# The base inverse of a gated delta-rule kernel: its DVE sections placed at other slots, and one ACT copy between two Silus

## The chip, the cores and the metric

One core of one Trainium2 chip runs the whole program. The time is that of one execution on the device, in microseconds, as the median of several runs. The engines are TensorE (PE, with its weight loads shown as PEld), VectorE (DVE), ScalarE (ACT), GpSimd (POOL) and SyncE (SP). Each has its own queue, runs it in order, and is tied to the others by semaphores alone.

## The reference, cut to what matters

The program is a block of four layers. Only the first, an attention layer with a gated delta rule over 32 value heads, is touched:

```python
mixed = silu(causal_conv4(x @ w_qkv))            # q, k: 16 heads; v: 32 heads
beta, g = sigmoid(x @ w_b), -exp(A_log) * softplus(x @ w_a + dt_bias)
def step(state, inp):                            # over 1024 tokens
    state = state * exp(g_t)
    delta = (v_t - k_t @ state) * b_t
    state = state + outer(k_t, delta)
    return state, q_t @ state
core = norm_w * rms(core) * silu(z)
return core @ w_out
```

A scan, two quantized feed-forward layers and a state-space layer follow (the last quarter of the time); the change leaves them alone.

## The kernel before

**Units and slots.** The layer is cut into 32 units (2 batches by 16 key heads, 2 value heads each) and each unit's 1024 tokens into 8 chunks of 128. A unit starts every 8 slots. `for slot in range(ATTENTION_SLOTS)` runs over 279 slots, and each engine's function (`tensor`, `scalar`, `vector`, `gpsimd`, `sync`) walks the same slots and issues what is due in each: a step of unit n that is written for unit slot k is issued in slot 8n+k. Several units are in flight, so a slot is known by its **position**, its number modulo 8; unit slots 9 and 17 both fall on position 1. In every slot there is one step of the scan over chunks (unit slots 16 to 23), up to three products of the projection ("a", "b", "c" in the code, L676) and one output product (L831).

**The scan's step in a slot.** PE multiplies key and state (L712); DVE makes the residual from it (`resid`, L1333); PE multiplies that with the triangular inverse (L780) to `u`, which ACT copies (L1046); PE makes the state's update and the output (L810, L814); DVE takes them into `state` (L1406) and `o` (L1417). At a unit's chunk 0 there is no residual and the copies are L1399 and L1414.

**The inverse.** Each unit needs the inverse of 8x2 triangular 128x128 tiles, in two halves a=0 and a=1. The 16x16 diagonal blocks are inverted on DVE by `base_inverse`: section 0 is four 32x32 transposes and four elementwise steps (L1167 to L1178), and then for each column j from 1 to 14 three short dependent instructions on 128 x 8j elements (shuffle L1186, multiply L1188, add L1190), with one more (L1194) at the end. POOL spreads the result over the blocks (`inv`, L1519, "the mask"). DVE turns that (`turn_base`, L1198), and PE takes it from there: L605, which waits for the mask, then L608, which waits for DVE's turned copy and for ACT's copy of L605's result (`off`, L1068), and further levels in the next slots, of which L617 waits for ACT's copies L1074/L1075.

**Where the sections stand before.** Half 0: section 0 at unit slot 10, columns 1 to 6 at 11 ahead of the state, columns 7 to 10 at the end of slot 11, columns 11 to 14 at the end of slot 12. Half 1: the same four slots later, with section 0 at the end of slot 14. So the last columns stand right ahead of the residual of position 5 (half 0) and of position 1 (half 1).

**Other work named below.** `evict_pair` (L1150, L1153) and `subtract` (L1371, in the old code inline) prepare the decay matrix; `gate_out` writes `oT` (L1291) after PE's transposes (L761); `convolve` is three passes of L1306 over 128x1024, which wait for ACT's first tap (L1008); L1277 on DVE and L910, L914 and L917 on ACT read the projection's products out of the banks. On POOL, L1460 sums weights, L1498 scales `o`, L1505 masks the decay and L1469 issues the output's DMA. In ACT's queue, positions 1 and 5 have a table load (L1016), two Silus (L888), the copies, a Silu on `z` (L1051), a table load back (L1052) and then L1068.

Of the kernel before, what the change touches and what calls it, by code (L numbers as in the profile page):

```python
# [13 lines left out]
P = 128  # L14
# [200 lines left out]
def attention(nc, ctx, c, banks, dram, x_in, x_out, early):  # L215
    on = signals(nc, ctx, ATTENTION_SIGNALS)
    with ExitStack() as st:
# [631 lines left out]
        def scalar(e):  # L849
# [92 lines left out]
            for slot in range(ATTENTION_SLOTS):  # L942
# [72 lines left out]
                if n_qk is not None or n_v is not None or n_z is not None:  # L1015
                    e.preload_act_table_set(SILU_SET)  # L1016
                    if n_qk is not None:
                        silu(n_qk, K)
                        silu(n_qk, Q)
                    if n_v is not None:  # L1020
                        silu(n_v, V0)
                        silu(n_v, V1)
                    if n_z is None:
                        e.preload_act_table_set(EXP_SET)

                if slot in (5, 6):
                    evict_rows(1, range(4 * (slot - 5), 4 * (slot - 4)))
                read_at(slot, "b")
# [109 lines left out]
        def vector(e):  # L1138
# [16 lines left out]
            def base_inverse(n, a, section):  # L1155
# [24 lines left out]
                for j in range(1, BASE - 1):  # L1180
                    if section == (1 if j < 7 else 2 if j < 11 else 3):
# [10 lines left out]
                if section == 3:  # L1192
# [101 lines left out]

            def convolve(slot, taps):
# [18 lines left out]
            for slot in range(ATTENTION_SLOTS):  # L1314
# [33 lines left out]

                for a in range(2):
                    n = unit_at_only(slot, 9 + 4 * a)  # L1350
                    if n is not None:
                        evict_pair(n, a, 0)
                for a in range(2):
                    n = unit_at_only(slot, 8 + a)
                    if n is not None:
                        N = n
                        if a == 0:
                            if N in (0, HK):
                                e.wait_ge(on["gates"], N // HK + 1)
                            e.wait_ge(on["ln"], N + 1)  # L1360
                            if N > 0:
                                e.wait_ge(on["decay_sub"], 2 * N)
                            norm = ln_norm[:, N % 3, K, :].unsqueeze(1).broadcast_to([P, REP, NC])
                            heads = slice(REP * (n % HK), REP * (n % HK + 1))
                            e.tensor_tensor(col_beta[:, :, :], gc_beta[:, n // HK, heads, :], norm, ALU.add).then_inc(
                                on["col_beta"], 1)
                        e.wait_ge(on["chunk_exp"], 2 * N + a + 1)
                        e.wait_ge(on["col_beta"], N + 1)
                        dec = decay_half(N, a)
                        col = col_beta[:, :, HALF * a:HALF * (a + 1)].unsqueeze(3).broadcast_to([P, REP, HALF, P])  # L1370
# [1083 lines left out]
```

## Time and profile before

| | us |
|---|---|
| median of 3 runs (lowest to highest) | 4165.66 (4164.44 to 4167.02) |
| the profiled execution | 4168.05 |
| its span, first to last instruction | 4166.1 |
| attention with both scan and projection running, one unit | 88.2 |
| PE busy / DVE / ACT / POOL in the span | 3997.3 / 3196.9 / 2592.6 / 958.8 |

Times in the trace are microseconds from the span's start. The unit whose slots are quoted below is typical: from the second unit to the last but one, a unit took 88.14 to 88.58 us, but for the second (88.36) and the thirtieth (87.82), and the steps stand at the same distances in each. The granted TensorE clock is 0.991 of full speed over the span.

### The profile page before, as it was taken

The page shows a single profiled execution, that of the slowest core. Times are in us where ns is not written, and L with a number is a line of the kernel's source. Part 1 is how long each engine was busy: PE and PEld are TensorE (multiplying, and loading weights), DVE is VectorE, ACT ScalarE, POOL GpSimd, SP SyncE. Part 2 cuts the span into 40 slices and gives each one's busy share as a digit, 9 for nine tenths or more (in the row PEclk, how much of TensorE's full clock was granted, in tenths as well). Part 3 has the DMA queues.
Part 4 walks back from the last instruction along what each step waited for, and adds up shares of the span by engine and source line. Part 5 has one row for each costly group of instructions (what it writes and reads, how often), then busy time and mean ns, then how long its engine had stood idle before and what let it go on. Part 6 is the DMA issues. An engine that isn't in the chain of part 4 may idle for free. (4 is left out here: it accounts for less than half of the span.)

```text
span 4166.1 us, 83038 instructions
## 1 busy us (share of the span) xinstructions
PE 3997.3 (96%) x29437; PEld 2282.0 (55%) x29437; DVE 3196.9 (77%) x8334; ACT 2592.6 (62%) x6087; POOL 958.8 (23%) x1110
## 2 busy tenths in 40 slices
PE   7999999999999999999999999998899999999999
PEld 4555556556555555566565555555444444444444
DVE  4777887787787777877778877777447989898940
ACT  3566676666666666666666666666445656574643
POOL 1224333234333243333333333332100000000000
PEclk9999999999999999999999999999999999999999
DMA  3223334333433433343334333334304545454510
GB/s 131 83 72 84 87 86 90 85 80 85 92 77 85 120 82 85 90 86 85 81 87 92 75 87 85 82 80 97 83 1 132 164 148 168 147 175 153 183 57 10
DMA packets 290733, 402.99 MB, mean 97 GB/s; under 512 B 25774, under 2 KB 125362, under 8 KB 290258
## 3 DMA queue, kind: packets, MB, share of 16 engines
q1 hardware_dynamic: 253458, 330.57, 26.1%
q0 software_dynamic: 36864, 67.13, 12.0%
q8 instruction: 236, 3.87, 0.4%
q14 instruction: 175, 1.43, 0.1%
HBM read 288.56 MB, written 113.25 MB: 96 GB/s over the span
## 5 line engine op out<-in xcount | busy, mean ns | idle before, releaser
L676 PE MATMUL bank<-x_blocks,rows_b 128*128 128x512 f32 x1536 | 713.0, 597 | 0.9 <-ACT partial L914 0.9
L1306 DVE SCALAR_TENSOR_TENSOR conv<-raw,conv_w,conv 128x1024 f32<-128x1024 f32 x384 | 522.7, 1361 | 61.9 <-ACT conv L1008 56.8
L676 PE MATMUL bank<-x_blocks,w_pair 128*128 128x512 f32 x1152 | 549.9, 605 | 14.8 <-DVE x_blocks L1277 4.5
L831 PE MATMUL bank<-w_out_unit,oT 128*128 128x512 f32 x1008 | 491.4, 610 | 0.9 <-ACT out_stage L931 0.9
L676 PEld LDWEIGHTS bank<-x_blocks,rows_b 128*128 128x128 f32 x1536 | 274.9, 190 | 249.1 <-issue 231.3
L1662 PE MATMUL bank<-xnT_f,w_gu 128*128 128x512 f32 x704 | 324.5, 605 | 1.2 <-ACT xnT_f L2161 0.9
L1291 DVE SCALAR_TENSOR_TENSOR oT<-bank,norm_w,z 128x256 f32<-128x256 f32 x252 | 119.2, 473 | 261.4 <-PE bank L761 260.3
L676 PEld LDWEIGHTS bank<-x_blocks,w_pair 128*128 128x128 f32 x1152 | 206.8, 193 | 205.5 <-issue 169.5
L2231 ACT ACTIVATE step_decay<-dt,rate 128x512 f32<-128x512 f32 x256 | 183.4, 720 | 217.1 <-DVE h L2340 215.0
L1681 PE MATMUL bank<-w_down,hidden 128*128 128x512 f32 x704 | 316.9, 594 | 1.7 <-DVE x_blocks L1740 1.7
L1671 PE MATMUL bank<-xnT_f,w_gu 128*128 128x512 f32 x704 | 316.8, 593 | 0.5 <-DVE hidden L1702 0.5
L1127 ACT ACTIVATE k_scaled<-o 128x128 f32<-128x128 f32 x512 | 154.0, 302 | 227.5 <-DVE o L1417 175.4
L1469 POOL DMA_DIRECT2D x_after<-out_stage x256 | 223.0, 904 | 149.8 <-ACT out_stage L931 144.6
L831 PEld LDWEIGHTS bank<-w_out_unit,oT 128*128 128x128 f32 x1008 | 173.1, 192 | 128.0 <-issue 121.9
L1519 POOL TENSOR_TENSOR inv<-n_base,slot_mask 128x512 f32<-128x512 f32 x64 | 81.5, 1274 | 647.7 <-DVE n_base L1194 647.7
L1188 DVE TENSOR_TENSOR rows_b<-rows_b 128x8 f32<-128x8 f32 (+13 forms) x896 | 200.2, 223 | 30.8
L1190 DVE TENSOR_TENSOR n_base<-n_base,rows_b 128x8 f32<-128x8 f32 (+13 forms) x896 | 199.7, 223 | 30.8
L931 ACT COPY out_stage<-bank 128x512 f32<-128x512 f32 x256 | 148.4, 580 | 108.4 <-PE bank L831 99.9
L1681 PEld LDWEIGHTS bank<-w_down,hidden 128*128 128x128 f32 x704 | 130.4, 191 | 152.0 <-issue 151.9
L1662 PEld LDWEIGHTS bank<-xnT_f,w_gu 128*128 128x128 f32 x704 | 132.7, 195 | 147.2 <-issue 145.7
L1671 PEld LDWEIGHTS bank<-xnT_f,w_gu 128*128 128x128 f32 x704 | 130.8, 191 | 149.9 <-issue 148.2
L1186 DVE STREAM_SHUFFLE rows_b<-n_base 128x8 f32<-128x8 f32 (+13 forms) x896 | 207.2, 231 | 0.0
(270 smaller groups left out, 8360.8 us busy)
## 6 DMA issues: line engine op xcount, KB each, us to landing
x_after<-out_stage POOLq DMA_DIRECT2D x256, 256.0 KB, 4.2
rows_b<-bc_rows SPq DMA_DIRECT2D x256, 256.0 KB, 3.6
rows_c<-bc_rows SPq DMA_DIRECT2D x256, 256.0 KB, 3.7
w_pair<-in_w_qkv SPq DMA_DIRECT2D x128, 256.0 KB, 3.9
decay<-gc_rows SPq DMA_DIRECT2D x64, 512.0 KB, 5.0
z<-z_rows SPq DMA_DIRECT2D x64, 512.0 KB, 5.1
z_rows<-x_blocks SPq DMA_DIRECT2D x96, 256.0 KB, 5.8
w_pair<-in_w_z SPq DMA_DIRECT2D x64, 256.0 KB, 3.3
```

Source lines behind the costliest of these rows:

```text
L676: made = e.matmul(bank[:, :], weight[:, j, :], part(0, m)[:, j, :], start=j == 0 and m in (1, 5), stop=j == 1, skip_group_check=True)
L831: made = e.matmul(out_rows(N, t)[:, :], turned_to(N, t)[:, r, :], w_out[:, N % 2, r, :], start=r == 0, stop=r == REP - 1)
L1127: made = e.activation(squares[:, r, :], o[:, at % O_RING, r, :], ACT.Square, accum_out=o_rstd[:, N % 2, t, r:r + 1])
L1186: e.stream_shuffle(row, cols, lanes).then_inc(on["base"], 1)
L1188: e.tensor_tensor(row, row, col, ALU.mult).then_inc(on["base"], 1)
L1190: e.tensor_tensor(cols, cols, row, ALU.add).then_inc(on["base"], 1)
L1306: e.scalar_tensor_tensor(acc, raw[:, i, tap:tap + T], conv_w[:, tap, col:col + 1], acc, ALU.mult, ALU.add).then_inc(on["conv"], 1)
L1469: e.dma_start(x_out[n // HK][t * P:(t + 1) * P, :], out_stage[:, at % STAGES, :], accum_op=ALU.add).then_inc(on[f"x_added{at % STAGES}"], 16)
L1662: made = e.matmul(GB[:, :], w_gu[:, j, i * P:(i + 1) * P], xnT[:, R % 2, j, :], start=j == 0, stop=j == KT - 1)
L1671: made = e.matmul(UB[:, :], w_gu[:, j, INNER + i * P:INNER + (i + 1) * P], xnT[:, R % 2, j, :], start=j == 0, stop=j == KT - 1)
L1681: made = e.matmul(DB[t][:, :], hidden[:, U % 2, t * P:(t + 1) * P], w_down[:, i, :], start=i == 0, stop=i == IT - 1)
L2231: e.activation(step_decay[:, (p + 2) % DECAY_RING, :], dt[:, (KT * q + i) % 2, :], ACT.Exp, scale=rate[:, i, n:n + 1]).then_inc(on["step_d ...
```

## The change

On **DVE** the columns are cut into four sections in place of three (columns 1 to 3, 4 to 6, 7 to 10, 11 to 14 and the end), and placed anew:

- section 0 stands behind the residual and ahead of the products' reads, at unit slots 10 and 14 (positions 2 and 6);
- columns 1 to 3 stand in the same place one slot later, columns 4 to 10 behind `gate_out` and ahead of the read "b" and of the state (positions 3 and 7);
- the last columns of half 0 stand behind the residual of unit slot 12 (position 4), those of half 1 behind the residual of unit slot 17 (position 1), one slot later than before;
- the second `subtract` (position 1) moves behind `turn_base` and `gate_out`.

On **ACT** the read of product "b" moves between the two Silus of positions 1 and 5. No instruction is added or removed, and PE's, POOL's and SP's order is as it was.

```diff
@@ scalar
                     if n_qk is not None:
                         silu(n_qk, K)
+                    if n_v is not None:
+                        silu(n_v, V0)
+                if slot in (5, 6):
+                    evict_rows(1, range(4 * (slot - 5), 4 * (slot - 4)))
+                read_at(slot, "b")
+                if n_qk is not None or n_v is not None or n_z is not None:
+                    if n_qk is not None:
                         silu(n_qk, Q)
                     if n_v is not None:
-                        silu(n_v, V0)
                         silu(n_v, V1)
...
-                read_at(slot, "b")
@@ vector
-                    if section == (1 if j < 7 else 2 if j < 11 else 3):
+                    if section == (1 if j < 4 else 2 if j < 7 else 3 if j < 11 else 4):
...
-                if section == 3:
+                if section == 4:
...
+                n = unit_at_only(slot, 17)
+                if n is not None:
+                    base_inverse(n, 1, 4)
                 for a in range(2):
                     n = unit_at_only(slot, 9 + 4 * a)
                     if n is not None:
                         evict_pair(n, a, 0)
...
+                subtract(slot, 0)
...
                         turn_base()
+                for a in range(2):
+                    for section, at in ((0, 10 + 4 * a), (1, 11 + 4 * a), (4, 12)):
+                        n = unit_at_only(slot, at)
+                        if n is not None and (section < 4 or a == 0):
+                            base_inverse(n, a, section)
                 read_at(slot, "a")
                 gate_out(slot)
-                n = unit_at_only(slot, 10)
-                if n is not None:
-                    base_inverse(n, 0, 0)
+                subtract(slot, 1)
                 convolve(slot, (2, 1))
                 for a in range(2):
                     n = unit_at_only(slot, 11 + 4 * a)
                     if n is not None:
-                        base_inverse(n, a, 1)
+                        base_inverse(n, a, 2)
+                        base_inverse(n, a, 3)
...
-                    n = unit_at_only(slot, 10 + 4 * a)
-                    if n is not None and a == 1:
-                        base_inverse(n, a, 0)
-                    n = unit_at_only(slot, 11 + 4 * a)
-                    if n is not None:
-                        base_inverse(n, a, 2)
-                    n = unit_at_only(slot, 12 + 4 * a)
-                    if n is not None:
-                        base_inverse(n, a, 3)
```

DVE's queue around the start of position 1, before (`n_base` with L1186 to L1194 is the base inverse; the rows of columns 11 to 14 are cut to the first and the last):

```order
L1306 SCALAR_TENSOR_TENSOR conv<-raw,conv_w,conv 128x1024
L1186 STREAM_SHUFFLE rows_b<-n_base 128x8x11
...
L1194 TENSOR_TENSOR n_base<-n_base,base_ident 128x128
L1333 SCALAR_TENSOR_TENSOR resid<-bank,e_gc,v_tok 128x128 x2
L1150 TENSOR_TENSOR lT<-bank,decay 128x512
L1153 TENSOR_TENSOR decay<-bank,decay 128x2x2x128
L1371 TENSOR_TENSOR decay<-decay,col_beta 128x2x512
L1198 STREAM_TRANSPOSE inv_turned<-inv 128x512
L1291 SCALAR_TENSOR_TENSOR oT<-bank,norm_w,z 128x256
```

and the same place now (two lines of code were added, so L1333 reads L1354 here, L1371 reads L1314, and the others are 2 higher but for L1306, now L1327):

```order
L1327 SCALAR_TENSOR_TENSOR conv<-raw,conv_w,conv 128x1024
L1354 SCALAR_TENSOR_TENSOR resid<-bank,e_gc,v_tok 128x128 x2
L1188 STREAM_SHUFFLE rows_b<-n_base 128x8x11
...
L1196 TENSOR_TENSOR n_base<-n_base,base_ident 128x128
L1152 TENSOR_TENSOR lT<-bank,decay 128x512
L1155 TENSOR_TENSOR decay<-bank,decay 128x2x2x128
L1200 STREAM_TRANSPOSE inv_turned<-inv 128x512
L1293 SCALAR_TENSOR_TENSOR oT<-bank,norm_w,z 128x256
L1314 TENSOR_TENSOR decay<-decay,col_beta 128x2x512
```

The residual went ahead of the twelve short column steps and of L1194, and the subtract behind `oT`.

DVE's queue at position 2, from the residual to the convolution, before:

```order
L1333 SCALAR_TENSOR_TENSOR resid<-bank,e_gc,v_tok 128x128 x2
L1277 TENSOR_TENSOR raw<-bank,partial 128x512
L1291 SCALAR_TENSOR_TENSOR oT<-bank,norm_w,z 128x256
L1167 STREAM_TRANSPOSE l_quads<-lT 32x256 x4
L1170 TENSOR_TENSOR rows_b<-l_quads,strict_even 128x128
```

and now:

```order
L1354 SCALAR_TENSOR_TENSOR resid<-bank,e_gc,v_tok 128x128 x2
L1169 STREAM_TRANSPOSE l_quads<-lT 32x256 x4
L1172 TENSOR_TENSOR rows_b<-l_quads,strict_even 128x128
L1173 TENSOR_TENSOR rows_b<-l_quads,strict_odd 128x128
L1178 TENSOR_TENSOR n_base<-rows_b 128x128
L1180 TENSOR_TENSOR rows_b<-rows_b 128x128
L1279 TENSOR_TENSOR raw<-bank,partial 128x512
L1293 SCALAR_TENSOR_TENSOR oT<-bank,norm_w,z 128x256
```

Section 0 went ahead of the read of product "a" and of `oT`.

ACT's queue at position 5, before and then now:

```order
L1016 ACT_TABLE_LOAD
L888 ACTIVATE kq<-conv 128x1024 x2
L910 COPY bank<-bank 128x512
L1046 ACTIVATE u<-bank 128x256
L1051 ACTIVATE z<-z 128x2x512
```

```order
L1016 ACT_TABLE_LOAD
L888 ACTIVATE kq<-conv 128x1024
L910 COPY bank<-bank 128x512
L888 ACTIVATE kq<-conv 128x1024
L1048 ACTIVATE u<-bank 128x256
L1053 ACTIVATE z<-z 128x2x512
```

The copy of product "b" went one Silu forward; what follows the Silus stands where it stood.

## Rows read from the trace of the kernel before

**Rows 1.** The page, busy time by engine: us, share of the span, instructions.
```profile
PE 3997.3 (96%) x29437; PEld 2282.0 (55%) x29437; DVE 3196.9 (77%) x8334; ACT 2592.6 (62%) x6087; POOL 958.8 (23%) x1110
```

**Rows 2.** Waits, whole span: engine line waited for: total us, times, longest.
```profile
PE bank L780 <- DVE resid L1333: 52.5, 64, 4.2
PEld bank L605 <- POOL inv L1519: 19.5, 62, 0.3
```

**Rows 3.** Timeline, position 1: start, duration, engine, line, operation [idle before <- by].
```profile
1499.84 0.61 PE L712 MATMUL bank<-state,kq 128*128 128x256 f32 x2
1499.94 1.27 DVE L1306 SCALAR_TENSOR_TENSOR conv<-raw,conv_w,conv 128x1024 f32<-128x1024 f32 x1
...
1505.00 0.60 DVE L1333 SCALAR_TENSOR_TENSOR resid<-bank,e_gc,v_tok 128x128 f32<-128x128 f32 x2
1505.17 1.27 POOL L1519 TENSOR_TENSOR inv<-n_base,slot_mask 128x512 f32<-128x512 f32 x1 [5.76 <-DVE n_base L1194]
...
1506.49 0.75 PE L605 MATMUL bank<-inv,lT 32*32 32x32 f32 x64
```

**Rows 4.** Timeline, end of position 4 and position 5.
```profile
1543.67 0.60 DVE L1406 SCALAR_TENSOR_TENSOR state<-state,chunk_decay,bank 128x128 f32<-128x128 f32 x2
...
1545.59 0.59 PE L712 MATMUL bank<-state,kq 128*128 128x256 f32 x2
...
1548.48 0.59 ACT L917 COPY raw<-bank 128x512 f32<-128x512 f32 x1 [0.58 <-PE bank L676]
...
1555.54 0.47 ACT L1068 ACTIVATE off<-bank,neg_odd 128x256 f32<-128x256 f32 x1
...
1556.16 0.74 PE L608 MATMUL bank<-off,inv_turned 32*32 32x32 f32 x64
```

**Rows 5.** Timeline, position 2.
```profile
1513.35 0.60 PE L712 MATMUL bank<-state,kq 128*128 128x256 f32 x2
...
1513.98 0.61 DVE L1333 SCALAR_TENSOR_TENSOR resid<-bank,e_gc,v_tok 128x128 f32<-128x128 f32 x2
...
1516.24 0.69 DVE L1277 TENSOR_TENSOR raw<-bank,partial 128x512 f32<-128x512 f32 x1 [1.65 <-PE bank L676]
1516.29 0.73 POOL L1460 TENSOR_TENSOR rows_b<-w_pair,rows_b 128x256 f32<-128x256 f32 x1 [0.22 <-PE bank L676]
...
1518.58 1.83 DVE L1167 STREAM_TRANSPOSE l_quads<-lT 32x256 f32<-32x256 f32 x4
...
1521.06 0.27 ACT L1075 ACTIVATE off<-bank 32x128 f32<-32x128 f32 x1
...
1521.51 1.28 DVE L1306 SCALAR_TENSOR_TENSOR conv<-raw,conv_w,conv 128x1024 f32<-128x1024 f32 x1
...
1522.14 0.22 PE L617 MATMUL bank<-invT,off 32*32 32x32 f32 x2
```

**Rows 6.** Timeline, position 7 into position 0: columns 4, 7; reads; PE's product "a".
```profile
1488.13 0.18 DVE L1186 STREAM_SHUFFLE rows_b<-n_base 128x32 f32<-128x32 f32 x1
...
1490.16 0.68 DVE L1277 TENSOR_TENSOR z_extra<-bank,partial 128x512 f32<-128x512 f32 x1
...
1491.10 0.22 DVE L1186 STREAM_SHUFFLE rows_b<-n_base 128x56 f32<-128x56 f32 x1
...
1491.57 1.88 PE L676 MATMUL bank<-x_blocks,w_pair 128*128 128x512 f32 x4
...
1494.22 0.17 DVE L1365 TENSOR_TENSOR col_beta<-gc_beta,ln_norm 128x16 f32<-128x16 f32 x1
```

**Rows 7.** Timeline, position 0: a POOL and a DVE step that overlap.
```profile
1584.06 1.09 POOL L1505 TENSOR_SCALAR_AFFINE_SELECT decay<-decay 128x1024 f32<-128x1024 f32 x1 [2.78 <-DVE decay L1371]
1584.23 3.36 DVE L1306 SCALAR_TENSOR_TENSOR conv<-raw,conv_w,conv 128x1024 f32<-128x1024 f32 x2
```

**Rows 8.** Timeline, the last unit's position 1, where DVE waits for the mask.
```profile
2894.49 0.71 DVE L1198 STREAM_TRANSPOSE inv_turned<-inv 128x512 f32<-128x512 f32 x1 [0.85 <-POOL inv L1519]
...
2895.60 1.90 POOL L1498 TENSOR_TENSOR o<-o,o_rstd 128x1024 f32<-128x1024 f32 x1
```

More of the change, by code:

```diff
@@ L1024, in scalar @@
                         e.preload_act_table_set(EXP_SET)
-                if slot in (5, 6):
-                    evict_rows(1, range(4 * (slot - 5), 4 * (slot - 4)))
-                read_at(slot, "b")
                 for b in range(B):
@@ L1293, in gate_out, with subtract @@
                             on["oT_copy"], 1)
+            def subtract(slot, a):
+                n = unit_at_only(slot, 8 + a)
+                if n is not None:
+                    if a == 0:
+                        if n in (0, HK):
+                            e.wait_ge(on["gates"], n // HK + 1)
+                        e.wait_ge(on["ln"], n + 1)
+                        if n > 0:
+                            e.wait_ge(on["decay_sub"], 2 * n)
+                        norm = ln_norm[:, n % 3, K, :].unsqueeze(1).broadcast_to([P, REP, NC])
+                        heads = slice(REP * (n % HK), REP * (n % HK + 1))
+                        e.tensor_tensor(col_beta[:, :, :], gc_beta[:, n // HK, heads, :], norm, ALU.add).then_inc(
+                            on["col_beta"], 1)
+                    e.wait_ge(on["chunk_exp"], 2 * n + a + 1)
+                    e.wait_ge(on["col_beta"], n + 1)
+                    dec = decay_half(n, a)
+                    col = col_beta[:, :, HALF * a:HALF * (a + 1)].unsqueeze(3).broadcast_to([P, REP, HALF, P])
+                    e.tensor_tensor(dec, dec, col, ALU.subtract).then_inc(on["decay_sub"], 1)
             def convolve(slot, taps):
@@ L1347, in vector @@
                     part_sums(1)
+                n = unit_at_only(slot, 17)
+                if n is not None:
+                    base_inverse(n, 1, 4)
                 for a in range(2):
@@ L1352, in vector @@
                         evict_pair(n, a, 0)
-                for a in range(2):
-                    n = unit_at_only(slot, 8 + a)
-                    if n is not None:
[L1356 to L1370, printed above, removed]
-                        e.tensor_tensor(dec, dec, col, ALU.subtract).then_inc(on["decay_sub"], 1)
+                subtract(slot, 0)
                 for a in range(2):
@@ L1432, in vector @@
                         turn_inverse(a)
-                    n = unit_at_only(slot, 10 + 4 * a)
-                    if n is not None and a == 1:
-                        base_inverse(n, a, 0)
-                    n = unit_at_only(slot, 11 + 4 * a)
-                    if n is not None:
-                        base_inverse(n, a, 2)
-                    n = unit_at_only(slot, 12 + 4 * a)
-                    if n is not None:
-                        base_inverse(n, a, 3)
         def gpsimd(e):
```

## The prediction, made before the changed kernel ran

> **What bounds the kernel now.** I read the page's busy times first: PE is busy for 3997 of 4166 us [rows 1], so only the times in which PE stands still can be won. The list of waits says who makes it stand. The largest entry is L780 waiting for DVE's residual, 64 times, 52.5 us in all; L605 waits for POOL's mask 62 times, 19.5 us [rows 2]. These two are what the change aims at. Then I read one unit in order of time. At position 1 DVE finishes the convolution at 1501.2, works through the last columns, and starts the residual only at 1505.00, though PE's L712 was done at 1500.45; the mask follows on POOL from 1505.17 to 1506.44, and L605 starts at 1506.49, 6.65 us after L712 [rows 3]. At position 5 the picture is the same with half 0, and the stretch ends with L608 at 1556.16, which needs ACT's L1068 (1555.54 to 1556.01) [rows 4]. So there are two waits in a row at each place, and the question for each is which one ends last once the first is gone.
>
> **Position 5 (half 0): the stall goes, the time doesn't.** The residual and the mask will both be early there: the last columns run a slot sooner. That takes some 0.5 us off L780's wait and 0.3 off L605's. But L608 stands behind them and waits for L1068, and L1068 is the end of a row of ACT work that starts with the copy L917 at 1548.48 and has no pause up to 1556.01: copy, table load, two Silus, copy, `u`, the Silu on `z`, table load, L1068. Its first step waited for PE's product, with 0.58 us of idle time before it [rows 4], and not for the residual. The change only swaps two members of that row. So L608 stays at 1556.16 and the gain is **0**. The move of the read "b" keeps PE's next product from waiting for it; it shortens nothing else. What would make this wrong is a gain of at most the two stalls, 0.8 us.
>
> **Position 1 (half 1).** Now the residual comes first, 0.63 us after L712 starts (the distance where DVE is free, [rows 5]), and takes 0.52 of DVE. The last columns took from 1501.15 to 1505.00 with the mask starting 4.03 us after their first step, and it takes 1.27 and 0.05 to L605 [rows 3]. So L605 comes 0.63+0.52+4.03+1.27+0.05 = 6.50 us after L712, against 6.65: **-0.15 us**. L780 no longer waits, L605 waits in its place. That holds if DVE is free by then. It is at work from position 7 on without rest before the change; after it, it reaches position 0 some 1.9 us sooner, since 12 column steps have gone ahead. If DVE were as late as now, the term would be +0.5.
>
> **Position 7 into 0.** Columns 4 to 10 now stand ahead of the read of product "b" (L1277). Columns 4 to 6 take 1490.16-1488.13 = 2.03, columns 7 to 10 take 1494.22-1491.10 = 3.12, in all 5.15 us in place of the 3.98 of columns 1 to 6, which began at 1486.18, so the read starts 1.17 later, at 1491.33, and is done at 1492.01. PE's next product "a" writes over that bank and started at 1491.57 [rows 6]. It will wait until 1492.06. Not all of the 0.5 us passes on, because PE waits 0.3 us for an ACT copy two steps later in any case; the same delay reaches ACT through `o`. Between 0 and 0.5, I take **+0.25 us**.
>
> **Position 2.** Section 0 goes ahead of the read of "a". It takes 1518.58 to 1521.51, 2.93 us, and starts now at 1513.98+0.52 = 1514.50, so it ends at 1517.43. The read stood at 1516.24, after 1.65 us of idle time [rows 5]; it comes 1.19 later, and ACT's first tap, which waits for it, with all that stands behind in ACT's queue: the read "b", `u`, the evictions of v, L1074 and L1075. The last of these ended at 1521.33, L617 started at 1522.14: 0.8 us of slack, and about 0.2 more in short pauses of ACT between them. The rest, **+0.2 us**, is a new wait of PE at L617. There is a second cost: POOL's L1460 runs from about 1516.3 to 1517.0, and now DVE's four steps with two SBUF inputs (L1170 to L1178) fall in that time. What such a meeting costs the trace shows at position 0: two passes of L1306 took 3.36 us where L1505 had begun 0.17 us before them [rows 7]; a pass alone takes 1.27 or 1.28 [rows 3, 5], so 0.75 of the 3.36 is waiting. Here the overlap is 0.6 us at most; I take **+0.45**, between 0 and 0.7.
>
> The Trainium skill states the mechanism ("SBUF — State Buffer", section "Who interferes with whom"): a DVE instruction with two SBUF inputs and a GpSimd instruction that reads SBUF share a port, and who issues first holds it for the whole instruction. The trace agrees, with the 0.75 us above. It speaks against this change: DVE's small steps are moved to where POOL works. Without this rule and its row the sum would lack 0.6 us a unit, 18 us in all, and come to that of the first rival below.
>
> **Position 4 into 5.** The last columns of half 0 now let POOL's mask (1.27) start while DVE begins its convolution, and POOL's weight sums follow it there instead of one slot later. By the row above the first pass loses some 0.8 us, and the second up to 0.7 more if a weight sum gets in first. The columns themselves delay `oT` by 0.2, since DVE had idled 3 us there. The state was done at 1544.27 and PE's L712 of position 5 started at 1545.59 [rows 4]: 1.3 us of slack against 1.0 or 1.7 of delay. So between 0 and +0.5, I take **+0.15**.
>
> **At no cost:** section 0 at position 6, in 1.9 us of waiting for PE's L761 and 1.0 for ACT's tap; columns 1 to 10 at position 3, which delay the state by 0.9 us with more than 1 us before the next L712; the subtract of position 1, whose readers on POOL are behind L1498 anyway. If the cover at position 3 were gone, it would cost those 0.9. The head and the drain (units at either end) I put at 0, give or take 2 us.
>
> **Sum.** -0.15+0.25+0.2+0.45+0.15 = +0.9 us a unit, times 30 full units = +27 us. The profiled execution would go from 4168.05 to 4195, the median from 4165.66 to **4193 us**.
>
> **The rivals.**
> 1. *No collisions bite.* Then a unit costs -0.15+0.25+0.2 = +0.3, in all +9 us or less: 4165 to 4175. For: POOL's steps are short, and many DVE steps beside them read a PSUM bank and were not slowed. Against: rows 7.
> 2. *The subtract loses a race at position 1.* L1371 (two SBUF inputs, 1.2 us) is now ready about 1.05 us after DVE's L1198 starts; POOL's L1498 (1.90 us) started 1.11 after it at the one place where both wait for the mask [rows 8]. If POOL comes first, DVE stands for 1.5 us, is 0.9 us late at position 2, and L617 waits that much longer (less the 0.45, since section 0 then misses L1460): +0.5 more a unit, +15: 4208, up to 4220. For: 0.1 us decides. Against: in rows 8 DVE is ahead by it.
> 3. *Faster: the stalls that go aren't taken again.* If L608 isn't really held by L1068 at position 5 but by DVE's turned copy or the mask, 0.8 us a unit are won there; with -0.15 at position 1 and little lost at 2 and 7, about -0.6 a unit, -18 us: 4148. It decides at 0.9 us a unit of new waits. For: L780's and L605's stalls are real and add up to 72 us. Against: ACT has no pause before L1068 [rows 4].
> 4. *DVE stays late* and position 1 costs +0.5: 4212.
>
> **How the numbers follow.** Forecast (4180 to 4206) 0.50; rival 1 0.20; rival 2 and 4 together 0.17; rival 3 0.13. Less than 0.2%, 8 us, is about what a measurement of this kernel tells from no change. Rival 1 lies mostly inside that. Faster 0.12, same 0.18, slower 0.70. The range leaves out rival 3 and the upper end of rival 2: 4163 to 4214.
>
> **What the profile after would show.** The wait of L780 for the residual nearly gone; L605's wait for POOL grown to about 1.5 us at position 1 and gone at position 5; at position 5 a wait of L608 for ACT's L1068 of about 1 us; at position 2 a wait of L617 for ACT, with DVE's L1277 1.2 to 1.7 us later; L676 waiting for L1277 at position 0; the unit at 89.1 us instead of 88.2. Wrong I would be most of all if L608 moved forward with the mask, or if L617 never waited.

## The result, and the profile after

The changed kernel takes 4205.72 us (median of 4 runs, 4204.10 to 4206.97), the kernel before, run beside it, 4165.05 us (4 runs, 4163.18 to 4167.02): a ratio of 1.0097, with a 95% interval of 1.0080 to 1.0115. It is slower by 40.7 us. The forecast was 4193 with a range of 4163 to 4214 and 0.70 for slower; so direction and range held, and the size came out 13 us above it. The profiled execution spans 4202.3 us, against 4166.1 before.

The page of the kernel after, busy time by engine: us, share of the span, instructions. It answers [rows 1].

```profile
PE 3981.7 (95%) x29437; PEld 2279.5 (54%) x29437; DVE 3248.8 (77%) x8334; ACT 2588.5 (62%) x6087; POOL 1042.0 (25%) x1110
```

PE does the same work in no more time. DVE is busy for 52 us more and POOL for 83 more, with no instruction more: each of their steps takes longer on average.

The waits of PE in the kernel after, whole span (engine, line, waited for: us in total, times, longest). They answer [rows 2]; L1070 and L1077 are the lines L1068 and L1075 of before, L1521 is L1519, L1279 is L1277.

```profile
PE bank L605 <- POOL inv L1521: 48.3, 32, 4.5
PE bank L608 <- ACT off L1070: 31.5, 31, 1.7
PE bank L617 <- ACT off L1077: 20.9, 31, 1.1
PE bank L676 <- DVE z_extra L1279: 13.6, 29, 0.7
```

L780's 52.5 us are gone from the head of the list. In their place stand four waits, one for each place that the prediction named. L605's wait is counted in [rows 2] for its weight load: 19.5 us in 62 pieces. Counted the same way it is 54.4 us in 32 pieces now, at position 1 alone.

How long does each position last? The next table has the stretches from one start of L712 to the next, as means over 24 units in the middle of the program, read from the starts of L712 in each trace.

| us | 1 to 2 | 2 to 3 | 3 to 4 | 4 to 5 | 5 to 6 | 6 to 7 | 7 to 1 | unit |
|---|---|---|---|---|---|---|---|---|
| before | 13.59 | 11.68 | 10.29 | 10.27 | 13.07 | 10.54 | 18.80 | 88.24 |
| after | 13.37 | 12.40 | 10.29 | 10.37 | 13.18 | 10.54 | 19.12 | 89.27 |
| difference | -0.22 | +0.72 | 0 | +0.10 | +0.11 | 0 | +0.32 | +1.03 |

(1 to 2 is the stretch from the L712 of position 1 to that of position 2, and 7 to 1 passes over position 0, where a unit's chunk 0 has no L712.)

One unit of the kernel after, its position 1, which answers [rows 3] (timeline: start, duration, engine, line, operation [idle before <- by]):

```profile
1516.31 0.59 PE L712 MATMUL bank<-state,kq 128*128 128x256 f32 x2
1516.94 0.61 DVE L1354 SCALAR_TENSOR_TENSOR resid<-bank,e_gc,v_tok 128x128 f32<-128x128 f32 x2 [0.42 <-PE bank L712]
...
1521.51 1.27 POOL L1521 TENSOR_TENSOR inv<-n_base,slot_mask 128x512 f32<-128x512 f32 x1 [6.67 <-DVE n_base L1196]
...
1522.83 0.75 PE L605 MATMUL bank<-inv,lT 32*32 32x32 f32 x64 [1.28 <-POOL inv L1521]
...
1523.81 1.21 DVE L1314 TENSOR_TENSOR decay<-decay,col_beta 128x1024 f32<-128x1024 f32 x1
...
1523.89 2.88 POOL L1500 TENSOR_TENSOR o<-o,o_rstd 128x1024 f32<-128x1024 f32 x1
```

The residual is no longer late: DVE had even idled 0.42 us for L712. The columns follow it, then the mask, then L605, 6.52 us after L712 where the prediction said 6.50. DVE's subtract began 0.08 us ahead of POOL's L1500, so the race of the second rival was won here by DVE, by less than the 0.1 us that the prediction spoke of. It was the same in all units from the third to the last but one: the subtract began 7.49 to 7.51 us after L712, and POOL's L1500 7.57 us after it or later.

Position 2 of the same unit, which answers [rows 5]:

```profile
1529.69 0.59 PE L712 MATMUL bank<-state,kq 128*128 128x256 f32 x2
...
1532.63 0.73 POOL L1462 TENSOR_TENSOR rows_b<-w_pair,rows_b 128x256 f32<-128x256 f32 x1 [0.22 <-PE bank L676]
1532.71 0.79 DVE L1172 TENSOR_TENSOR rows_b<-l_quads,strict_even 128x128 f32<-128x128 f32 x1
...
1534.27 0.68 DVE L1279 TENSOR_TENSOR raw<-bank,partial 128x512 f32<-128x512 f32 x1
...
1534.99 1.15 ACT L1008 ACTIVATE conv<-raw,conv_w 128x1024 f32<-128x1024 f32 x1 [2.99 <-DVE raw L1279]
...
1539.20 0.22 PE L617 MATMUL bank<-invT,off 32*32 32x32 f32 x2 [0.65 <-ACT off L1077]
```

The read L1279 starts 4.58 us after L712; before it was 2.89 after it. ACT stands for 2.99 us until the read is done, and L617 waits for ACT. Within section 0, L1172 took 0.79 us beside POOL's L1462. Its sister L1173, of the same shape, took 0.28. So it is in 28 of the 30 units after the first; in the thirteenth L1172 began 0.12 us ahead of POOL's step and took 0.29, and L1173 took 0.81 in its place.

Position 0 of the same unit, which answers [rows 6]: the read now ends last before PE's product "a".

```profile
1507.60 0.68 DVE L1279 TENSOR_TENSOR z_extra<-bank,partial 128x512 f32<-128x512 f32 x1
...
1508.34 1.98 PE L676 MATMUL bank<-x_blocks,w_pair 128*128 128x512 f32 x4 [0.47 <-DVE z_extra L1279]
```

Position 4 into 5, and the end of position 5, which answer [rows 4]:

```profile
1557.81 3.78 DVE L1327 SCALAR_TENSOR_TENSOR conv<-raw,conv_w,conv 128x1024 f32<-128x1024 f32 x2
...
1560.64 1.53 POOL L1462 TENSOR_TENSOR rows_b<-rows_b,w_pair 128x256 f32<-128x256 f32 x1
...
1562.75 0.30 PEld L712 LDWEIGHTS bank<-state,kq 128*128 128x128 f32 x2 [0.35 <-DVE state L1416]
1562.76 0.70 PE L712 MATMUL bank<-state,kq 128*128 128x256 f32 x2
...
1565.75 0.58 ACT L917 COPY raw<-bank 128x512 f32<-128x512 f32 x1 [0.48 <-PE bank L676]
...
1568.03 0.75 PE L605 MATMUL bank<-inv,lT 32*32 32x32 f32 x64
...
1572.82 0.47 ACT L1070 ACTIVATE off<-bank,neg_odd 128x256 f32<-128x256 f32 x1
...
1573.44 0.74 PE L608 MATMUL bank<-off,inv_turned 32*32 32x32 f32 x64 [0.99 <-ACT off L1070]
```

L605 comes 5.27 us after L712 with no wait, and still L608 comes 10.68 us after L712; before it was 10.57. The stall moved behind L605 and became 0.99 us long. ACT's row, which ends in L1070, began 2.99 us after L712 (L917) and not 2.89 as before: that is the 0.1 us by which L608 is later. The two passes of the convolution took 3.78 us. In the kernel before, the same two passes ran undisturbed in 2.60 (timeline of the kernel before, position 4):

```profile
1540.55 2.60 DVE L1306 SCALAR_TENSOR_TENSOR conv<-raw,conv_w,conv 128x1024 f32<-128x1024 f32 x2
```

The weight load of the next L712 now waits 0.35 us for the state.

### The profile page after: what moved, and what is told of

Same layout as the page of the kernel before. It is cut to its first block and busy times, and to the rows that moved or that the text cites. A ratio compares the mean times of both kernels' runs of the same rounds, so it can differ in the third digit from the quotient of the medians.

```text
span 4202.3 us, 83038 instructions
## 1 busy us (share of the span) xinstructions
PE 3981.7 (95%) x29437; PEld 2279.5 (54%) x29437; DVE 3248.8 (77%) x8334; ACT 2588.5 (62%) x6087; POOL 1042.0 (25%) x1110
## 5 line engine op out<-in xcount | busy, mean ns | idle before, releaser
L676 PE MATMUL bank<-x_blocks,rows_b 128*128 128x512 f32 x1536 | 712.9, 597 | 0.9 <-ACT partial L914 0.9
L1327 DVE SCALAR_TENSOR_TENSOR conv<-raw,conv_w,conv 128x1024 f32<-128x1024 f32 x384 | 537.6, 1400 | 81.8 <-ACT conv L1008 76.7
L676 PE MATMUL bank<-x_blocks,w_pair 128*128 128x512 f32 x1152 | 553.5, 608 | 28.6 <-DVE z_extra L1279 13.6
L676 PEld LDWEIGHTS bank<-x_blocks,rows_b 128*128 128x128 f32 x1536 | 274.4, 190 | 249.5 <-issue 231.7
L676 PEld LDWEIGHTS bank<-x_blocks,w_pair 128*128 128x128 f32 x1152 | 204.7, 191 | 225.6 <-issue 163.2
L1129 ACT ACTIVATE k_scaled<-o 128x128 f32<-128x128 f32 x512 | 154.2, 303 | 211.0 <-DVE o L1427 194.2
L1471 POOL DMA_DIRECT2D x_after<-out_stage x256 | 222.3, 870 | 245.9 <-ACT out_stage L931 237.4
L1354 DVE SCALAR_TENSOR_TENSOR resid<-bank,e_gc,v_tok 128x128 f32<-128x128 f32 x448 | 136.0, 345 | 185.7 <-PE bank L712 181.6
L1192 DVE TENSOR_TENSOR n_base<-n_base,rows_b 128x8 f32<-128x8 f32 (+13 forms) x896 | 213.5, 238 | 30.8
L1462 POOL TENSOR_TENSOR rows_b<-w_pair 128x256 f32<-128x256 f32 x192 | 174.7, 910 | 244.3 <-PE bank L676 238.4
L931 ACT COPY out_stage<-bank 128x512 f32<-128x512 f32 x256 | 148.4, 580 | 115.2 <-PE bank L831 104.8
L1008 ACT ACTIVATE conv<-raw,conv_w 128x1024 f32<-128x1024 f32 x128 | 150.0, 1172 | 99.4 <-DVE raw L1279 99.4
```

What stands on the lines that cost most here:

```text
L676: made = e.matmul(bank[:, :], weight[:, j, :], part(0, m)[:, j, :], start=j == 0 and m in (1, 5), stop=j == 1, skip_group_check=True)
L1129: made = e.activation(squares[:, r, :], o[:, at % O_RING, r, :], ACT.Square, accum_out=o_rstd[:, N % 2, t, r:r + 1])
L1192: e.tensor_tensor(cols, cols, row, ALU.add).then_inc(on["base"], 1)
L1327: e.scalar_tensor_tensor(acc, raw[:, i, tap:tap + T], conv_w[:, tap, col:col + 1], acc, ALU.mult, ALU.add).then_inc(on["conv"], 1)
L1462: e.tensor_tensor(w_sums[:, at, :, :], first, second, op).then_inc(on["w_sum"], 1)
L1471: e.dma_start(x_out[n // HK][t * P:(t + 1) * P, :], out_stage[:, at % STAGES, :], accum_op=ALU.add).then_inc(on[f"x_added{at % STAGES}"], 16)
```

## The experiments

The theory under test (where a text on record gives it a letter, A) is the prediction's sum with the sizes of the table above: every new wait is real, each sits in its own stretch, and each has the cause that the prediction gave. Each text says itself what its rivals expect. The runs undo the parts one at a time, then put together what was left, and two are made from the kernel before. All medians stand beside the kernel before run on the same chip, at 4164 to 4167 us; that kernel's own median moves by 3 us between these sets of runs, so a difference of two medians from different sets, as to the changed kernel's 4205.72, is uncertain by as much. The seven stretches, in which the granted clock is 1.00, are not.

### Section 0 behind the read again

```diff
                         n = unit_at_only(slot, at)
-                        if n is not None and (section < 4 or a == 0):
+                        if n is not None and (section < 4 or a == 0) and (section, a) != (0, 0):
                             base_inverse(n, a, section)
                 read_at(slot, "a")
                 gate_out(slot)
                 subtract(slot, 1)
+                n = unit_at_only(slot, 10)
+                if n is not None:
+                    base_inverse(n, 0, 0)
                 convolve(slot, (2, 1))
```

> The changed kernel, but section 0 of half 0 (unit slot 10, position 2) back behind the read of product a and oT. Theory A (read a, and with it ACT's row up to L1077, is late only because section 0 stands ahead of it): the stretch from position 2 to 3, 12.40 us now, returns to 11.68; the unit goes from 89.27 to 88.55, the time from 4206 to about 4184. Rival (DVE is late at position 2 because of position 1): the wait of L617 for ACT stays at 0.5 us or more and the time at 4200 or above.

Measured: 4185.65 us, a ratio of 1.0054 (1.0038 to 1.0071). The stretch 2 to 3 is back at 11.68 us, the unit 88.55. The wait L617 on ACT is gone from the list, and the others stand as they were. Timeline of this kernel, position 2:

```profile
1521.65 0.59 PE L712 MATMUL bank<-state,kq 128*128 128x256 f32 x2
...
1524.54 0.69 DVE L1279 TENSOR_TENSOR raw<-bank,partial 128x512 f32<-128x512 f32 x1 [1.65 <-PE bank L676]
1524.58 0.73 POOL L1465 TENSOR_TENSOR rows_b<-w_pair,rows_b 128x256 f32<-128x256 f32 x1 [0.21 <-PE bank L676]
```

The read is again 2.89 us after L712, beside POOL's step: it has one of its inputs in a PSUM bank, and neither of the two was slowed. So half of the loss of the change is where section 0 was put.

### The collision alone

```diff
+    later = m == 3 and pair % PAIRS == V_PAIR
-    e.wait_ge(on["product"], PRODUCTS * (pair - 1) + max(ORDER.index(m), ORDER.index(5)) + 1)
+    e.wait_ge(on["product"], PRODUCTS * (pair - 1) + max(ORDER.index(m), ORDER.index(5)) + 1 + later)
```

The order of DVE stays that of the change. POOL's one weight sum waits for one product more, so that it begins after section 0.

> The changed kernel, but one weight sum of POOL (of the three pairs' sums the one that ran beside L1172 at position 2) waits for one product more and so runs 1.6 us later. It measures the collision by itself. Theory A: L1172 takes 0.29 us again in place of 0.79, the read of product a comes 0.5 sooner, L617's wait falls from 0.8 to 0.3, the unit from 89.27 to about 88.8, the time to about 4192. Rival (the lateness is all section 0's own length): L1172 is short again, but L617 waits as before and the time stays at 4206.

Measured: 4194.57 us (one run); the stretch 2 to 3 is 11.90 us, 0.50 less than after, the unit 88.77. The time is 11 us lower than the changed kernel's where 30 units give 15: in this execution the first unit and the last full one were longer by 2 and 3 us. Timeline of this kernel, position 2:

```profile
1528.06 0.29 DVE L1172 TENSOR_TENSOR rows_b<-l_quads,strict_even 128x128 f32<-128x128 f32 x1
...
1529.12 0.68 DVE L1279 TENSOR_TENSOR raw<-bank,partial 128x512 f32<-128x512 f32 x1
1529.69 0.73 POOL L1463 TENSOR_TENSOR rows_b<-w_pair,rows_b 128x256 f32<-128x256 f32 x1 [1.94 <-PE bank L676]
...
1534.05 0.22 PE L617 MATMUL bank<-invT,off 32*32 32x32 f32 x2 [0.16 <-ACT off L1077]
```

With POOL's step out of the way L1172 takes 0.29 us again, the read comes 4.09 instead of 4.58 us after L712, and L617's wait falls from 0.65 to 0.16. The two terms of position 2 are thereby separated: 0.50 for the collision, 0.22 for the order.

### Last columns of half 1 not ahead of `o`

```diff
     base_inverse(n, a, 2)
-    base_inverse(n, a, 3)
+    if a == 0:
+        base_inverse(n, a, 3)
...
     turn_inverse(a)
+    n = unit_at_only(slot, 15)
+    if n is not None:
+        base_inverse(n, 1, 3)
```

> The changed kernel, but columns 7 to 10 of half 1 (unit slot 15, position 7) back behind the read b and o, at the slot's end. Theory A: PE's wait for L1279 at the next product (0.47 us) goes, the stretch from position 7 to 1 goes from 19.12 to about 18.8, and the drain, where the same steps stand ahead of o with nothing beside them, gives 2 to 4 us back: time about 4193. Rival: DVE is then late for the residual of position 1 as in the kernel before, the residual's stall is back there, and nothing is won (4203 or above).

Measured: 4190.01 us, 1.0064 (1.0049 to 1.0079); the stretch 7 to 1 is 18.79 us, the unit 88.94, and the wait of L676 for DVE's read is no longer among the longest of its list. This term is +0.33. The run is 15.7 us faster than the change, of which 30 units give 9.9. A part of the rest is in the drain: the last stretch from a position 7 to the next L712 took 13.99 us, against 17.23 after and 11.95 before. Timeline of the kernel after, that place:

```profile
2920.40 0.42 DVE L1427 TENSOR_TENSOR o<-bank,q_state 128x256 f32<-128x256 f32 x1
2920.85 0.31 ACT L1129 ACTIVATE k_scaled<-o 128x128 f32<-128x128 f32 x1 [2.15 <-DVE o L1427]
...
2921.57 0.59 ACT L931 COPY out_stage<-bank 128x512 f32<-128x512 f32 x1
...
2922.21 0.69 PE L761 MATMUL bank<-ident,o 128*128 128x128 f32 x2 [4.04 <-ACT out_stage L931]
```

The projection's products (L676) are over there, so PE has nothing to do while DVE works off columns 4 to 10 (2915.12 to 2920.48) ahead of `o`. ACT's L1129 waits for `o`, the copy L931 stands behind it in ACT's queue, and PE's L761 waits for that copy: PE stands for 4.04 us. In the kernel before, L761 waited 1.79 us for the same copy at this place, and in this run again 1.79; so the order costs 2.25 us here. In the middle of the program it costs 0.33, because the projection's products run beside it.

The rest of the 17.23 us is the TensorE clock. From L761 to the next L712, in the kernel before and then after (window, its length; busy us of PE, PEld, DVE, ACT and POOL, with their instructions; granted clock, DMA share, GB/s):

```profile
2886.27:2890.35 4.08, 3.61 (x18) 2.47 (x19) 3.46 (x17) 1.95 (x9) 0.00 (x0) 1.00 0.00 0
```
```profile
2922.20:2928.95 6.75, 6.27 (x18) 4.32 (x19) 1.33 (x3) 1.95 (x9) 0.00 (x0) 0.54 0.00 0
```

The same 18 instructions of PE took 6.27 us in place of 3.61, at a granted clock of 0.54: mostly the lower of its two levels, 1.2 GHz and not 2.4. Here the clock fell right behind the 4.04 us in which PE stood. In this run with the columns moved the same stretch took 5.76 us at a clock of 0.70. The kernel before has such a stretch at half the clock too, but a slot later, from 2895.50 to 2902.30.

### Last step of half 1 a slot sooner

```diff
-    n = unit_at_only(slot, 17)
-    if n is not None:
-        base_inverse(n, 1, 4)
...
     turn_inverse(a)
+    n = unit_at_only(slot, 16)
+    if n is not None:
+        base_inverse(n, 1, 4)
```

> The changed kernel, but the last columns of half 1 at the end of unit slot 16, ahead of the residual of position 1, as in the kernel before. Theory A: with DVE no longer late there, the old order is the better one: the columns start about 1.0 us sooner, L605 about 1.0 sooner; ACT's L1070 then ends last, and lets 0.4 to 0.5 us of it through: position 1 to 2 from 13.37 to about 12.95, time about 4192. Rival (the idea of the change holds: the columns behind the residual are better): L780's stall for the residual comes back at 1 us and the time is 4206 or more.

Measured: 4189.50 us, 1.0062 (1.0047 to 1.0077); the stretch 1 to 2 is 13.04 us (expected 12.95), the unit 88.95. First entry of the waits of this kernel:

```profile
PE bank L608 <- ACT off L1070: 52.8, 62, 1.7
```

The wait for the mask is gone, and L608 now waits for ACT at both positions, 62 times. So the mask hid an ACT wait at position 1, as the residual had hidden the mask: three waits in a row. With the mask's wait gone the stretch shrinks by 0.33 us only; the run with all four edits, where the ACT wait is gone too, has 12.35 us there, another 0.69 less.

### ACT's order of before

```diff
                         silu(n_qk, K)
-                    if n_v is not None:
-                        silu(n_v, V0)
-                if slot in (5, 6):
-                    evict_rows(1, range(4 * (slot - 5), 4 * (slot - 4)))
-                read_at(slot, "b")
-                if n_qk is not None or n_v is not None or n_z is not None:
-                    if n_qk is not None:
                         silu(n_qk, Q)
                     if n_v is not None:
+                        silu(n_v, V0)
                         silu(n_v, V1)
...
+                if slot in (5, 6):
+                    evict_rows(1, range(4 * (slot - 5), 4 * (slot - 4)))
+                read_at(slot, "b")
+
                 for b in range(B):
```

> The changed kernel with ACT's part undone: read b behind both Silus. Theory A (ACT's row to L1070 ends last at position 5 in either order): PE waits 0.5 us for L910 at product c and 0.5 us less at L608; the unit stays at 89.27 within 0.1 and the time at 4206. Rival (the copy between the Silus is worth its place): position 5 to 6 grows by 0.5 and the time by 15 us, to 4220.

Measured: 4210.36 us (one run). All seven stretches agree with those of the change to 0.01 us. Waits of this kernel:

```profile
PE bank L676 <- ACT bank L910: 17.8, 35, 1.5
...
PE bank L608 <- ACT off L1068: 9.3, 31, 1.7
```

The copy L910 between the Silus spares PE a wait of its next product, and L608 then waits longer instead: without it PE waits 17.8 us for the copy and 9.3 for L1068, with it 31.5 for L1070. The end of ACT's row is the same either way, so this part of the change is worth nothing in a unit as it stands. The 4.6 us by which this one run is longer than the changed kernel aren't in the units: in its profiled execution the first L712 comes 2.6 us later than in the changed kernel's, and the first and the last full unit are 1.6 and 2.8 us longer. Nothing tells whether the edit or chance does that.

### The copies of the inverse ahead of the `z` Silu

```diff
-                if n_z is not None:
-                    e.wait_ge(on[f"z_load{a_z}"], 16 * (n_z + 1))
-                    z_half = z[:, :, a_z * BANK:(a_z + 1) * BANK]
-                    e.activation(z_half, z_half, ACT.Silu).then_inc(on["z_silu"], 1)
-                    e.preload_act_table_set(EXP_SET)
-
                 n = unit_at_only(slot, 6)
                 if n is not None:
...
                         e.mul(off[hp:P, 1::2, :], inv_ps[0:hp, 1::2, :], -1.0).then_inc(on["inv_act"], 1)
 
+                if n_z is not None:
+                    e.wait_ge(on[f"z_load{a_z}"], 16 * (n_z + 1))
...
+                    e.preload_act_table_set(EXP_SET)
+
                 read_at(slot, "c")
```

> The changed kernel, but at positions 1 and 5 ACT does the Silu on z and the table load back after L1070 and not ahead of it. Theory A (at position 5 L1070 ends last, behind table load, Silus and the z Silu, and holds L608): L608 comes 1.1 us sooner at position 5, nothing changes at position 1, where POOL's mask ends last; position 5 to 6 from 13.18 to about 12.1, the unit from 89.27 to 88.2, the time to about 4173. Rival (something else, DVE's turned copy or the bank, ends last at position 5): no change, 4206.

Measured: 4174.25 us (median of 10 runs), 1.0018 (1.0009 to 1.0028). The stretch 5 to 6 is 12.13 us, 1.05 less than after, and the unit 88.23. Timeline of this kernel, position 5:

```profile
1548.96 0.70 PE L712 MATMUL bank<-state,kq 128*128 128x256 f32 x2
...
1556.67 0.46 ACT L1064 ACTIVATE off<-bank,neg_odd 128x256 f32<-128x256 f32 x1
1557.02 1.05 ACT L1083 ACTIVATE z<-z 128x1024 f32<-128x1024 f32 x1
1558.09 1.28 ACT L1084 ACT_TABLE_LOAD   x1
1558.58 0.75 PE L608 MATMUL bank<-off,inv_turned 32*32 32x32 f32 x64
```

L608 starts 9.62 us after L712 and waits for nothing. This shows the prediction's reason for the zero at position 5: what held the stretch was ACT's Silu and table load ahead of L1068, 2.3 us of work that PE didn't need.

### The same edit in the kernel before

> The kernel before, with ACT's copies of the product (L1068 to L1070) put ahead of the z Silu and of the load of the exponential table, which change nothing else. Theory: in the kernel before, L608 at position 5 waits for ACT, but so little behind the inverse that ended last there that only the reserve beyond it can be had: position 5 shrinks from 13.07 to about 12.8 us (the inverse of DVE becomes the last to end), the unit from 88.24 to about 88.0, the time to about 4158. Rival: ACT's row is the whole of the wait at position 5 also in the kernel before; then the stretch falls by 1 us as in the changed kernel, to about 12.1, and the time to about 4135.

Measured: 4157.29 us (median of 10 runs) against 4167.13, 0.9978 (0.9969 to 0.9988); the stretch 5 to 6 is 12.93 us, the unit 88.09. Expected were 12.8, 88.0 and 4158. The same edit that brings 1.05 us a unit in the changed kernel brings 0.14 here. That makes 4 of the 10 us won; the others lie at the ends, and that the time came out at the expected 4158 is luck. First entry of the waits of this kernel, and its position 5:

```profile
PE bank L780 <- DVE resid L1333: 51.4, 66, 2.6
```
```profile
1542.30 0.59 PE L712 MATMUL bank<-state,kq 128*128 128x256 f32 x2
...
1547.54 0.71 PE L780 MATMUL bank<-resid,invT 128*128 128x128 f32 x4 [0.45 <-DVE resid L1333]
...
1552.72 0.75 PE L608 MATMUL bank<-off,inv_turned 32*32 32x32 f32 x64
```

Here the late residual stalls L780 and all that PE does behind it, and L608 follows 0.15 us sooner than it did. So the two limits of position 5 lay 0.14 us apart. Taking away only one of them brings nothing (the change) or 0.14 (this run); both together bring 13.07 - 12.13 = 0.94.

### Only the last columns of half 1, in the kernel before

```diff
     part_sums(1)
+    n = unit_at_only(slot, 17)
+    if n is not None:
+        base_inverse(n, 1, 3)
...
-    n = unit_at_only(slot, 12 + 4 * a)
-    if n is not None:
+    n = unit_at_only(slot, 12)
+    if n is not None and a == 0:
         base_inverse(n, a, 3)
```

> The kernel before with one part of the change alone: the last columns of half 1 behind the residual of unit slot 17. Theory A (DVE, still late there, puts the 0.52 us of the residual ahead of the mask): L605 comes 0.5 us later, the unit goes from 88.24 to 88.75, the time from 4164 to about 4180. Rival (the residual's place itself is the gain that position 1 shows): position 1 to 2 shrinks as in the changed kernel, by 0.2 us, and the time falls to 4158.

Measured: 4185.43 us (one run; expected 4180). The stretch 1 to 2 is 14.07 us, 0.48 more than before; the others stay. First entry of the waits, and position 1:

```profile
PE bank L605 <- POOL inv L1522: 66.8, 32, 4.5
```
```profile
1507.67 0.61 PE L712 MATMUL bank<-state,kq 128*128 128x256 f32 x2
...
1508.97 0.60 DVE L1333 SCALAR_TENSOR_TENSOR resid<-bank,e_gc,v_tok 128x128 f32<-128x128 f32 x2
...
1513.52 1.26 POOL L1522 TENSOR_TENSOR inv<-n_base,slot_mask 128x512 f32<-128x512 f32 x1 [6.28 <-DVE n_base L1194]
```

Without the earlier columns, DVE is late at position 1 (the residual starts 1.30 us after L712, and 0.63 after it in the changed kernel), and the turned order costs 0.48 instead of winning 0.22. That is the fourth rival's condition, made on purpose, and its price of +0.5. The 5 us above the expectation lie mostly in the drain, 71.78 us for the last full unit against 67.25 before. Of these, 3.00 are in its last stretch, 14.95 us against 11.95: PE stood for 2.44 us in both, and the granted clock was 0.77 against 1.00.

### All four together

Section 0 behind the read, the last columns of half 1 at the end of slot 15, its last step at the end of slot 16, and the copies ahead of the `z` Silu, in the changed kernel.

> All together: section 0 of half 0 late, columns 7 to 10 of half 1 late, the last columns of half 1 ahead of the residual, L1070 ahead of the z Silu. Theory A adds up: -0.72 -0.33 -1.0 (ACT no longer caps it) -1.1 on 89.27 gives a unit of 86.1 and a time of about 4105, 60 us below the kernel before. Rival (a next limit, DVE late for a residual or ACT late for u, takes it back): a unit of 87 or more, 4130 or above.

Measured: 4104.83 us (median of 4 runs), 0.9852 (0.9837 to 0.9867): 60 us faster than the kernel before, and 101 us faster than the changed one. The stretches are 12.35, 11.68, 10.30, 10.37, 12.12, 10.54 and 18.79 us, the unit 86.15. One unit each of before, after and this kernel, from the L712 of position 7 to the next one (busy us of PE, PEld, DVE, ACT and POOL with their instructions, granted clock, DMA share, GB/s):

```profile
1481.05:1569.19 88.14, 86.16 (x809) 52.53 (x808) 70.35 (x210) 60.09 (x159) 30.68 (x34) 1.00 0.38 85
```
```profile
1497.18:1586.47 89.29, 85.86 (x810) 52.58 (x809) 72.17 (x210) 59.98 (x159) 32.38 (x34) 1.00 0.39 84
```
```profile
1452.91:1539.07 86.16, 85.84 (x809) 52.42 (x808) 72.71 (x210) 59.98 (x159) 32.06 (x34) 1.00 0.39 87
```

PE is busy for about 86 us in each; it stands still for 2.0, 3.4 and 0.3 us. In the best version 0.3 us a unit is all that is left to win by order in the middle of the program. In their own runs the four edits gave 0.72, 0.33, 0.33 and 1.05, in all 2.43 us a unit; together they give 89.27 - 86.15 = 3.12. The other 0.69 is at position 1, where two of them had to come together. Note that DVE is busier there than in either of the others: it doesn't bound the kernel, only its order against PE does.

## Why the prediction was right, point by point

- **Position 1:** forecast -0.15. L605 came 6.52 us after L712 (6.50 forecast, 6.65 before), and the stretch is 0.22 shorter; where the other 0.09 comes from was not traced. The condition, that DVE be free by then, held; the run with the last columns moved in the kernel before has +0.48 where DVE is late.
- **Position 7 into 0:** forecast +0.25; measured +0.32 in the table and 0.33 when undone. L676 started at 1508.34 behind a read that began at 1507.60, as forecast; a little more of the 0.47 us passed on than I took.
- **Position 2:** forecast +0.2 for the order and +0.45 for the collision; measured 0.22 and 0.50, by separate runs. The read came 4.58 us after L712 instead of 2.89, 1.69 later, where the sum of 1.19 and 0.45 gives 1.64. The mechanism is the one taken from [rows 7]: two steps that both read SBUF only, one after the other. One figure of it was read wrong: 3.36 less two passes of 1.27 and 1.28 is 0.81, not 0.75; by the pair that took 2.60 it is 0.76, so the forecast doesn't change by it.
- **Position 4 into 5:** forecast +0.15 between 0 and 0.5; measured +0.10. The two passes lost 1.18 us (3.78 against 2.60), and nearly all of it fell into the slack ahead of L712.
- **Position 5:** forecast 0; measured +0.11. L608 stayed behind ACT's L1070, whose row began 0.1 us later. Moving the copies ahead of the Silu gave 1.05 us there in the changed kernel. The third rival, a gain of 0.8 there, failed on its condition and not on its size: the stall was worth 12.93 - 12.13 = 0.80 us once ACT's row was shortened. (The prediction's 0.8 adds a wait of PE's weight load at L605 to one of PE at L780, and so do its 72 us; PE's own list of before has no wait at L605.) What I left out is that it needed only one move of ACT's order.
- **Moves put at no cost:** the stretches 3 to 4 and 6 to 7 are unchanged to 0.01 us.
- **The sum:** forecast +0.9 a unit, measured +1.03, each term off by 0.11 at most. That gives 31 us for 30 units instead of 27.
- **The mis-sized term: head and drain,** put at 0, give or take 2. By the profiled executions (+36.2 us in all) the 28 middle units have +28.9. The first L712 comes 1.1 later, the first unit is 1.1 longer, the next to last full unit 3.0, the last 4.4, and what follows is 2.4 shorter: +7.3, or about +5 more than two ordinary units would give. Two causes can be read. One is the order: L761's wait in the last unit is 2.25 us longer than before, since the columns ahead of `o` have the projection's products as cover in every unit but the last. The prediction read the cover in the unit only. The other is the granted clock, which is 1.00 in the middle and falls for short times in the drain, at other places in each execution. Behind L761's wait it cost 2.7 us. In the stretch 7 to 1 of the next to last full unit it was 0.84 against 0.91 before: PE was busy for 17.98 us against 16.48 there, with as many instructions, and stood 0.8 us longer. In the last unit's scan, from its position 1 to its last L712, it was 0.96 against 0.88, and that part is 1.6 us shorter. The same kernel can so come out some us longer or shorter at its ends; the first L712 alone lay between 181.7 and 186.8 us in the eleven profiled executions. The medians differ by 4.5 us more than the profiled executions do; that is the spread between executions.
- **The rivals:** no collisions (4165 to 4175) fell with L1172 at 0.79 us; the lost race of the subtract didn't occur (DVE ahead by 0.08 us); a margin of 0.08 us kept its +15 away, which is as much luck as foresight; DVE late fell with its 0.42 us of idle time ahead of the residual.

The Trainium skill ("SBUF — State Buffer", section "Who interferes with whom") says that a DVE instruction with two SBUF inputs and a GpSimd instruction that reads SBUF exclude each other for the whole instruction. Four measurements agree in kind: L1172 0.79 against 0.29 us, the passes of L1327 3.78 against 2.60, POOL's L1500 2.88 against 1.90, and the run in which only POOL's step was put later, which gave back the 0.50. In size one differs: POOL's L1462 ended at 1533.36 and L1172 at 1533.50, only 0.14 us later, though it needs 0.29; so by this row some 0.15 us of the two overlap: the exclusion ended before the recorded end of POOL's step, or a part of L1172's 0.29 us isn't subject to it. Here the measurement decides, and the row doesn't tell which.

## What to carry to other kernels

Where an engine waits, list the waits that stand behind it in the same stretch, and how far apart their ends are. Here they were the residual, the mask and ACT's copies. The change took the first away at both positions (-0.22 us at one, nothing at the other), moving the mask gave 0.33 and moving the copies in the kernel before 0.14, while everything together gave 2.09 us a unit. Removing the longest stall in the list gained 0.22 us a unit at most until the third one, which the list of before didn't show, went with it. A step that is moved earlier pays at its new place: ask what is queued behind it there, what reads SBUF beside it, and whether the cover it has in the steady part is there in the drain. At the ends, read the granted clock beside the waits before a difference is put down to an edit.

## What the runs showed of the hardware

- POOL pays too, 83 us over the whole program. POOL's L1500 takes 1.90 us alone and took 2.88 where DVE's subtract of 1.21 us had begun 0.08 us before it. PE's list of waits has no entry for L1500.
- An exclusion costs less than the overlap that the trace shows: L1172 began with 0.65 us of POOL's step left, and lost 0.50.
- Behind a pause of 4.04 us, 18 instructions of PE took 6.27 us at a granted clock of 0.54, against 3.61 us at 1.00 behind a pause of 1.79. In two executions in which PE stood for 2.44 us in the same stretch, the stretch took 11.95 us at 1.00 and 14.95 at 0.77.
- A step of POOL right behind its issue of a DMA is recorded longer: L1462 with the same input took 1.01 to 1.12 us each time that it stood behind L1471, and 0.71 to 0.78 the other times (times from 500 to 2700 us, about 74 of each). But its record begins before that of the issue ends: L1471 ran from 1530.77 to 1531.65 and L1462 from 1531.38 to 1532.41, so it ended 0.76 us behind the issue. The issue may well cost the step nothing; that was not tested.
